# The third layer of a graph network gathers the rows of x itself, instead of reading a copy stored by slot

## The chip, the cores and the metric

The kernel runs on one core of a Trainium2 chip. The metric is the time on the device in microseconds (us), the median of several runs. A core has five engines, each with its own instruction queue, which run side by side and wait for one another through semaphores: TensorE (PE; its weight loads are listed as PEld), VectorE (DVE), ScalarE (ACT), GpSimd (POOL) and SyncE (SP, which here only issues transfers). Transfers between HBM and the on-chip memory (SBUF) are issued by SP, or, where rows are picked by a list of indices, by POOL as indirect transfers.

## The reference

Three layers of a graph convolution over 20000 nodes with 512 features, 5000 edges sorted by destination, with a residual from layer to layer and from the input:

```python
h = x
residual = 0.0
for Wl, bl, Wr, g, b in params:                 # three layers
    msg = h[src]                                # 5000 rows
    s = segment_sum(msg, dst, 20000)
    cnt = segment_sum(ones, dst, 20000)
    agg = s / maximum(cnt, 1)
    h = residual + agg @ Wl.T + bl + h @ Wr.T
    h = layer_norm(h, g, b)                     # eps 1e-5
    h = where(h >= 0, h, a_prelu * h)
    residual = h
out = layernorm(x + h)                          # no gain or shift
```

## The kernel before

The nodes are renumbered into slots so that nodes that receive edges come first. There are 157 tiles of 128 slots; 40 of them receive messages. Two tiles make a unit, and a layer has 79 units: 59 plain ones and 20 edge units. In each layer 20 plain units come first; then an edge unit and two plain units alternate; one plain unit of a single tile comes last. The three layers run one behind the other as 237 turns of one pipeline, and every engine's program is a loop over the turn T that works on units somewhat ahead of or behind T. The order on each engine is thus written out by hand.

For unit u, TensorE transposes the rows (`turn`, into `ps_t`), and multiplies them as a sum of a high and a low part with split weights: 12 products of 128x512 a tile, and 12 more for a tile that gets messages (`product_self`, `product_mean`, L411). ScalarE takes the high part (`take_high`, L524), fills the accumulators with the bias (`fill`, L553), squares the result (`square`, L533) and forms the variance (`variance`, L543). POOL takes the inverse root (`root`, L690). VectorE takes the low part (`take_low`, L790), applies root and gain (`normal`, L801), adds the shift (`add_shift`, L822) and takes the PReLU (`prelu`, L828). For edge units it also builds comparison matrices (`compare`, L837 and L839), carries sums over tile borders (`carry`, L854) and takes low parts of sums (`take_sum_low`, L862). `normal` of a unit frees its accumulator, which `fill` and then TensorE need two units later.

In layer 3 the output follows. Tile `o_sb` (a ring of 6 buffers of two tiles) holds rows of x; VectorE adds the layer's result to them (`out_sum`, L870, three turns behind TensorE) and forms the mean (`out_mean`); ScalarE squares (`out_square`, L579); POOL's `root` handles the variance of this second normalisation in the same instruction, then forms `omove` (L694); ScalarE normalises (`out_norm`, L586); and POOL scatters the rows to the output, one indirect transfer a tile (`put_out`, L702).

In layer 1 the rows of x come by indirect transfers on POOL, one a tile (`gather_x`, L656), into `hin`. SP stores each unit from `hin` into the HBM tensor `x_by_slot` (`store_x`, L281); POOL waits for that store before it fills the buffer again. In layer 3 SP loads the unit's rows of `x_by_slot` into `o_sb` in one transfer (`load_residual`, L319), once the scatters that read that buffer six units before have landed (`o_put`). SP's order in a turn is `store_x`, `load_h`, `load_residual`, `load_rowtab`, `store_h`. POOL's order in turn T is: `root` (which waits for the variance), `omove`, the scatters of unit T-5, `gather_x` of unit T+3, the message gathers of unit T+3 if it is an edge unit (`gather_messages`, L679), and in layers 1 and 2 the small transfers that build the slot tables.

Of the kernel before, what the change touches and what calls it, by code (L numbers as in the profile page):

```python
# [7 lines left out]
P = 128  # L8
ALU = mybir.AluOpType
ACT = mybir.ActivationFunctionType  # L10
F32 = mybir.dt.float32
# [4 lines left out]
L = 3  # L16
# [6 lines left out]
def reach(eng, sem, count):  # L23

    if count > 0:
        eng.wait_ge(sem, count)  # L26


def build_program(nc, x, wT, bl, g, b, a_prelu, ident_in, const_in, edge_cols_in, edge_last_in, edge_rows_in,
                  edge_no_in, out):  # L30
    N, D = x.shape
# [3 lines left out]
    NT = -(-(N + ET) // P)  # L35
# [5 lines left out]
    UL = len(edge_units) + len(plain_units)  # L41
# [32 lines left out]
    def uses(ring, n, below):  # L74

        return len(range(ring, below, n))

    h_dram = [nc.dram_tensor(f"h{l + 1}_scratch", [NT * P, D], F32).ap() for l in range(L - 1)]
    xp_dram = nc.dram_tensor("x_by_slot", [NT * P, D], F32).ap()
    node_dram = nc.dram_tensor("node_of_rank", [EP, 1], I32).ap()  # L80
    slot_dram = nc.dram_tensor("slot_of_node", [NT * P, 1], I32).ap()
    rowtab_dram = nc.dram_tensor("edge_row_table", [ET, 2 * P], F32).ap()
# [1 line left out]
    with ExitStack() as ctx:  # L84
# [3 lines left out]
        def sem(name):  # L88
            return ctx.enter_context(nc.semaphore(name))


        OB = 6
# [19 lines left out]
        hin = [sb(f"hin{i}", [P, 2, D]) for i in range(3)]  # L112
# [23 lines left out]
        node_get = sb("node_get", [P, NT], I32)  # L136
# [83 lines left out]
        SRC_AHEAD = 6  # L220
# [3 lines left out]
        def stats(T):  # L224
# [19 lines left out]

        x_in = [[sem(f"x_in{i}_{j}") for j in range(2)] for i in range(3)]
        h_in = [sem(f"h_in{i}") for i in range(3)]
        xp_stored = [sem(f"xp_stored{i}") for i in range(3)]
        h_stored = [sem(f"h_stored{i}") for i in range(3)]
        turned, high, low, z_ready = sem("turned"), sem("high"), sem("low"), sem("z_ready")
        squared, veps_done, rstd_done = sem("squared"), sem("veps_done"), sem("rstd_done")  # L250
# [2 lines left out]
        m_in = [sem(f"m_in{j}") for j in range(2)]  # L253
        e_same, e_summed, e_carry, e_high, e_low = (
            sem("e_same"), sem("e_summed"), sem("e_carry"), sem("e_high"), sem("e_low"))
        xr_in = [sem(f"xr_in{i}") for i in range(OB)]
        o_put = [[sem(f"o_put{i}_{j}") for j in range(2)] for i in range(OB)]
        o_summed, o_mean, o_squared = sem("o_summed"), sem("o_mean"), sem("o_squared")
        o_move, o_done = sem("o_move"), sem("o_done")
# [1 line left out]
        def rows(dram, u):  # L261
            return dram[P * u.tiles[0]:P * (u.tiles[0] + u.n), :].rearrange("(j p) d -> p j d", p=P)


        def sync_program(sp):
            def load_weight(w):
                if w == 1:
                    sp.wait_ge(turned, 1)
                if w > 0:
                    sp.wait_ge(w_low, KC * w)  # L270
                sp.dma_start(stage[:], wT[w].rearrange("(c p) k -> p c k", p=P)).then_inc(stage_in, 16)

            def spread(vector, count):
                return vector.rearrange("(a d) -> a d", a=1).to_broadcast([count, vector.shape[0]])

            def store_x(u):
                if u.l > 0:
                    return
                for j in range(u.n):
                    sp.wait_ge(x_in[u.r3][j], 16 * (u.no // 3 + 1))  # L280
                sp.dma_start(rows(xp_dram, u), hin[u.r3][:, 0:u.n, :]).then_inc(xp_stored[u.r3], 16)  # L281

            def load_h(u):
                if u.l == 0:
                    return
                source = u.no - UL
                sp.wait_ge(turned, u.no - 2)
                sp.wait_ge(h_stored[source % 3], 16 * (source // 3 + 1))
                if u.no - 3 < UL:
                    sp.wait_ge(xp_stored[u.r3], 16 * uses(u.r3, 3, UL))  # L290
                sp.dma_start(hin[u.r3][:, 0:u.n, :], rows(h_dram[u.l - 1], u)).then_inc(h_in[u.r3], 16)

            def load_rowtab(u):
                if not u.edge:
                    return
                if u.eno == 0:
                    sp.wait_ge(rowtab_stored, 16)
                reach(sp, e_same, 2 * u.eno)
                t = u.tiles[0]
                pair = rowtab_dram[t:t + 2, :].rearrange("(a t) c -> a (t c)", a=1)  # L300
                sp.dma_start(rowtab[:].rearrange("p j c e -> p (j c e)"),
                             pair.to_broadcast([P, 4 * P])).then_inc(rt_in, 16)

            def store_h(u):
                if u.l == L - 1:
                    return
                sp.wait_ge(h_done, u.no + 1)
                sp.dma_start(rows(h_dram[u.l], u), hout[u.r3][:, 0:u.n, :]).then_inc(h_stored[u.r3], 16)

            def load_residual(u):  # L310
                if u.l < L - 1:
                    return
                if u.pos == 0:
                    sp.wait_ge(z_ready, NT)
                    for r in range(3):
                        sp.wait_ge(xp_stored[r], 16 * uses(r, 3, UL))
                for j in range(2):
                    reach(sp, o_put[u.ring][j], 16 * u.lap)
                sp.dma_start(o_sb[u.ring][:, 0:u.n, :], rows(xp_dram, u)).then_inc(xr_in[u.ring], 16)  # L319

            sp.dma_start(edge_cols[:], edge_cols_in).then_inc(cols_in, 16)
            sp.dma_start(const[:], const_in).then_inc(const_in_sem, 16)
            sp.dma_start(ident[:], ident_in).then_inc(ident_in_sem, 16)
            load_weight(0)
            sp.dma_start(edge_rows, edge_rows_in).then_inc(rows_in, 16)
            sp.dma_start(edge_no, edge_no_in).then_inc(rows_in, 16)
            sp.dma_start(dlast[:], spread(edge_last_in, P)).then_inc(rows_in, 16)
            for l in range(L):
                sp.dma_start(bias_rows[:, l, :], spread(bl[l], P)).then_inc(bias_in, 16)
            sp.dma_start(slope[:], spread(a_prelu, P)).then_inc(affine_in, 16)  # L330
            for l in range(L):
                sp.dma_start(gain[:, l, :], spread(g[l], P)).then_inc(affine_in, 16)
                sp.dma_start(shift[:, l, :], spread(b[l], P)).then_inc(affine_in, 16)
            sp.wait_ge(table_done, 1)
            sp.dma_start(node_dram.rearrange("(t p) c -> t (p c)", p=P), table_int[0:ET, 0, :]).then_inc(node_stored, 16)

            for T in range(-5, UNITS + 3):
                for stage_, ahead in ((store_x, 2), (load_h, 3), (load_residual, -1), (load_rowtab, 5), (store_h, -3)):
                    u = Unit(T + ahead)
                    if u.exists:  # L340
                        stage_(u)
                for w, at in W_SLOT.items():
                    if T == at - 4:
                        load_weight(w)
                if T == ROW_SLOT + 2:
                    sp.wait_ge(row_step, 12)
                    sp.dma_start(rowtab_dram, rows_out.rearrange("t c p -> t (c p)")).then_inc(rowtab_stored, 16)
                if T == TABLE_SLOT + 2:
                    sp.wait_ge(table_done, 3)
                    sp.dma_start(slot_dram[0:P * P, :].rearrange("(t p) c -> t (p c)", p=P),  # L350
                                 table_int[:, 0, :]).then_inc(slot_stored, 16)
                    sp.dma_start(slot_dram[P * P:NT * P, :].rearrange("(t p) c -> t (p c)", p=P),
                                 table_int[0:NT - P, 1, :]).then_inc(slot_stored, 16)
# [285 lines left out]
        def gpsimd_program(pool):  # L639
# [8 lines left out]
            def gather_x(u):  # L648
                if u.l > 0:
                    return  # L650
                reach(pool, turned, u.no - 2)
                reach(pool, xp_stored[u.r3], 16 * (u.no // 3))
                if u.edge:
                    pool.wait_ge(nodes_known, 2 + u.tiles[-1] // BATCH)
                for j, t in enumerate(u.tiles):
                    pool.indirect_dma_start(hin[u.r3][:, j, :], None, x,  # L656
                                            bass.IndirectOffsetOnAxis(node_get[:, t:t + 1], 0)).then_inc(x_in[u.r3][j], 16)

            def find_source(u):
                if not u.edge or u.l != 1:  # L660
# [47 lines left out]
            for T in range(-3, UNITS + 6):  # L708
# [2 lines left out]
                old = Unit(T - 5)  # L711
                if old.exists:
                    put_out(old)
                for stage_, ahead in ((gather_x, 3), (gather_messages, 3), (find_source, SRC_AHEAD)):
                    u = Unit(T + ahead)
                    if u.exists:
                        stage_(u)
# [22 lines left out]
        def vector_program(dve):  # L740
# [123 lines left out]
            def out_sum(u):  # L864
                if u.l < L - 1:
                    return
                dve.wait_ge(xr_in[u.ring], 16 * (u.lap + 1))
                dve.wait_ge(h_done, u.no + 1)
                for j in range(u.n):
                    nc.vector.scalar_tensor_tensor(o_sb[u.ring][:, j, :], hout[u.r3][:, j, :], sign[:, 0:1], o_sb[u.ring][:, j, :],  # L870
                                                   ALU.mult, ALU.add, accum_out=osum[u.ring][:, j:j + 1]).then_inc(o_summed, 1)

# [193 lines left out]
```

## Time and profile before

| what | value |
|---|---|
| median of 3 runs | 2023.56 us (2023.55 to 2024.12) |
| profiled execution | 2023.93 us, of which the span is 2022.1 |
| busy share of the span | PE 98%, PEld 82%, DVE 79%, ACT 60%, POOL 46% |
| TensorE in the 40 slices of the span | 90% busy or more in slices 2 to 39 |
| `gather_x` on POOL (L656) | 157 calls, mean 1001 ns, 3.8 us from issue to landing |
| `put_out` on POOL (L702) | 157 calls, mean 1039 ns, 2.9 us from issue to landing |
| store of a unit into `x_by_slot` | 512 KB, 3.3 us from issue to landing |
| load of a unit from `x_by_slot` | 512 KB, 4.6 us from issue to landing |

A "busy" engine is one with an instruction in hand. The idle time in front of an instruction is given with what ended it (`<-`). "Issue" is idle time in which the engine waited for nothing the profile shows. Layer 1 takes about the first 695 us, layer 2 the time to about 1335, layer 3 the rest.

### The profile page before, as it was taken

The page shows a single profiled execution, that of the slowest core. Times are in us where ns is not written, and L with a number is a line of the kernel's source. Part 1 is how long each engine was busy: PE and PEld are TensorE (multiplying, and loading weights), DVE is VectorE, ACT ScalarE, POOL GpSimd, SP SyncE. Part 2 cuts the span into 40 slices and gives each one's busy share as a digit, 9 for nine tenths or more (in the row PEclk, how much of TensorE's full clock was granted, in tenths as well). Part 3 has the DMA queues.
Part 4 walks back from the last instruction along what each step waited for, and adds up shares of the span by engine and source line. Part 5 has one row for each costly group of instructions (what it writes and reads, how often), then busy time and mean ns, then how long its engine had stood idle before and what let it go on. Part 6 is the DMA issues. An engine that isn't in the chain of part 4 may idle for free. (4 is left out here: it accounts for less than half of the span.)

```text
span 2022.1 us, 30522 instructions
## 1 busy us (share of the span) xinstructions
PE 1978.4 (98%) x10207; PEld 1659.0 (82%) x10207; DVE 1597.5 (79%) x2598; ACT 1221.7 (60%) x2667; POOL 926.7 (46%) x885
## 2 busy tenths in 40 slices
PE   8999999999999999999999999999999999999993
PEld 7888888888888888888888888887788888888882
DVE  7778777777777677777777777779999988888884
ACT  6865554554444455444444444458887777777774
POOL 3666656555565312332222333214555555555554
PEclk9999999999999999999999999999999999999997
DMA  6667667666666555544444444456666666656652
GB/s 209 226 232 258 215 219 233 221 208 214 204 204 207 161 162 183 170 146 152 146 145 151 157 156 144 138 173 216 221 230 217 211 212 213 209 203 218 214 183 92
DMA packets 181075, 387.69 MB, mean 192 GB/s; under 512 B 20117, under 2 KB 20562, under 8 KB 180918
## 3 DMA queue, kind: packets, MB, share of 16 engines
q1 hardware_dynamic: 142358, 272.06, 39.7%
q0 software_dynamic: 38560, 113.67, 17.3%
q8 instruction: 82, 1.34, 0.3%
q14 instruction: 75, 0.61, 0.1%
HBM read 221.07 MB, written 164.79 MB: 191 GB/s over the span
## 5 line engine op out<-in xcount | busy, mean ns | idle before, releaser
L411 PE MATMUL ps_z<-w_hi,hT_hi 128*128 128x512 f32 x1884 | 762.9, 405 | 5.7 <-ACT ps_z L553 4.9
L411 PE MATMUL ps_z<-w_hi,hT_lo 128*128 128x512 f32 x1884 | 738.6, 392 | 0.0
L411 PE MATMUL ps_z<-w_lo,hT_hi 128*128 128x512 f32 x1884 | 737.8, 392 | 0.0
L690 POOL TENSOR_TENSOR rstd<-veps,minus_half 128x2 f32<-128x2 f32 (+1 forms) x240 | 241.6, 1007 | 876.1 <-ACT veps L543 876.0
L790 DVE TENSOR_TENSOR hT_lo<-ps_t,hT_hi 128x1024 fp32r<-128x1024 f32 (+1 forms) x237 | 288.0, 1215 | 320.3 <-ACT hT_hi L524 317.6
L553 ACT COPY ps_z<-bias_rows 128x512 f32<-128x512 f32 x471 | 276.7, 588 | 346.5 <-DVE y L801 334.7
L533 ACT ACTIVATE junk<-ps_z 128x512 f32<-128x512 f32 x471 | 278.6, 592 | 322.3 <-PE ps_z L411 322.1
L411 PEld LDWEIGHTS ps_z<-w_hi,hT_lo 128*128 128x128 f32 x1884 | 353.4, 188 | 79.0
L411 PEld LDWEIGHTS ps_z<-w_hi,hT_hi 128*128 128x128 f32 x1884 | 354.4, 188 | 75.9 <-issue 8.1
L411 PEld LDWEIGHTS ps_z<-w_lo,hT_hi 128*128 128x128 f32 x1884 | 354.8, 188 | 66.9
L801 DVE SCALAR_TENSOR_TENSOR y<-ps_z,rstd,gain 128x512 f32<-128x512 f32 x471 | 330.2, 742 | 4.5 <-POOL rstd L690 4.5
L828 DVE SCALAR_TENSOR_TENSOR hout<-y,slope 128x1024 f32<-128x1024 f32 (+1 forms) x237 | 301.4, 1272 | 0.0
L822 DVE TENSOR_TENSOR y<-y,shift 128x1024 f32<-128x1024 f32 (+1 forms) x237 | 290.5, 1226 | 8.1
L391 PEld LDWEIGHTS ps_t<-ident,hin 128*128 128x128 f32 x1884 | 219.1, 140 | 34.2 <-issue 4.6
L391 PE MATMUL ps_t<-ident,hin 128*128 128x128 f32 x1884 | 244.7, 273 | 0.5 <-DVE hT_lo L790 0.5
L524 ACT CAST hT_hi<-ps_t 128x1024 fp32r<-128x1024 f32 (+1 forms) x237 | 234.7, 990 | 6.2 <-PE ps_t L391 5.9
L702 POOL DMA_INDIRECT out<-o_sb,node_put x157 | 163.1, 1039 | 68.2 <-issue 53.0
L411 PE MATMUL ps_z<-w_hi,sT_lo 128*128 128x512 f32 x480 | 188.0, 392 | 0.0
L411 PE MATMUL ps_z<-w_hi,sT_hi 128*128 128x512 f32 x480 | 187.7, 391 | 0.0
L411 PE MATMUL ps_z<-w_lo,sT_hi 128*128 128x512 f32 x480 | 187.7, 391 | 0.0
L656 POOL DMA_INDIRECT hin<-in_x,node_get x157 | 157.2, 1001 | 63.5 <-issue 36.2
L586 ACT ACTIVATE o_sb<-o_sb,omove,rstd 128x512 f32<-128x512 f32 x157 | 119.6, 809 | 68.5 <-POOL omove L694 68.5
(144 smaller groups left out, 1928.9 us busy)
## 6 DMA issues: line engine op xcount, KB each, us to landing
h_scratch<-hout SPq DMA_DIRECT2D x156, 512.0 KB, 3.7
hin<-h_scratch SPq DMA_DIRECT2D x156, 512.0 KB, 3.9
x_by_slot<-hin SPq DMA_DIRECT2D x78, 512.0 KB, 3.3
o_sb<-x_by_slot SPq DMA_DIRECT2D x78, 512.0 KB, 4.6
rowtab<-edge_row_table SPq DMA_DIRECT2D x60, 256.0 KB, 3.6
stage<-in_WrT SPq DMA_DIRECT2D x3, 1024.0 KB, 8.2
stage<-in_WlT SPq DMA_DIRECT2D x3, 1024.0 KB, 7.4
hin<-in_x,node_get POOLq DMA_INDIRECT x157, 3.8
```

The source lines that it names most:

```text
L391: mm = pe.transpose(ps_t[:, j, k * P:(k + 1) * P], hin[u.r3][:, j, k * P:(k + 1) * P], ident[:])
L411: mm = pe.matmul(acc, a[:, k, :], ww[:, k, :], start=False, skip_group_check=True, stop=stop and k == KC - 1 and a is a_lo)
L524: nc.scalar.copy(hT_hi[u.r2][:, 0:u.n].rearrange("p j k n -> p (j k n)"), ps_t[:, 0:u.n, :].rearrange("p j d -> p (j d)")).then_inc(high, 1)
L533: nc.scalar.activation(junk[j][:], ps_z[u.r2][:, j, :], ACT.Square, accum_out=ssq[u.r2][:, j:j + 1]).then_inc(squared, 1)
L553: nc.scalar.copy(ps_z[u.r2][:, j, :], bias_rows[:, u.l, :]).then_inc(filled, 1)
L656: pool.indirect_dma_start(hin[u.r3][:, j, :], None, x, bass.IndirectOffsetOnAxis(node_get[:, t:t + 1], 0)).then_inc(x_in[u.r3][j], 16)
L690: nc.gpsimd.tensor_tensor(rstd[(T - 1) % 2][:, at], veps[(T - 1) % 2][:, at], minus_half[:, at], ALU.pow).then_inc(rstd_done, 1)
L702: pool.indirect_dma_start(out, bass.IndirectOffsetOnAxis(node_put[:, t:t + 1], 0), o_sb[u.ring][:, j, :], None, bounds_check=N - 1, oob_is ...
L790: nc.vector.tensor_tensor(hT_lo[u.r2][:, 0:u.n].rearrange("p j k n -> p (j k n)"), ps_t[:, 0:u.n, :].rearrange("p j d -> p (j d)"), hT_hi[ ...
L801: nc.vector.scalar_tensor_tensor(y[u.r2][:, j, :], ps_z[u.r2][:, j, :], rstd[u.r2][:, j:j + 1], gain[:, u.l, :], ALU.mult, ALU.mult).then_ ...
L822: nc.vector.tensor_tensor(y[u.r2][:, 0:u.n, :], y[u.r2][:, 0:u.n, :], moved, ALU.add).then_inc(shifted, 1)
L828: nc.vector.scalar_tensor_tensor(hout[u.r3][:, 0:u.n, :], y[u.r2][:, 0:u.n, :], slope[:, 0:1], y[u.r2][:, 0:u.n, :], ALU.mult, ALU.max).th ...
```

## The change

The HBM copy `x_by_slot` is gone: SP no longer stores x in layer 1 and no longer loads it in layer 3, and POOL's gather of layer 1 no longer waits for a store. In layer 3 POOL gathers the unit's rows straight from the input into `o_sb`, one indirect transfer a tile, in turn T for unit T, after the scatters of the turn and ahead of its message gathers. Each tile of a buffer has a semaphore of its own, for which `out_sum` waits tile by tile.

```diff
-            def store_x(u):
-                if u.l > 0:
-                    return
-                for j in range(u.n):
-                    sp.wait_ge(x_in[u.r3][j], 16 * (u.no // 3 + 1))
-                sp.dma_start(rows(xp_dram, u), hin[u.r3][:, 0:u.n, :]).then_inc(xp_stored[u.r3], 16)
...
-                if u.no - 3 < UL:
-                    sp.wait_ge(xp_stored[u.r3], 16 * uses(u.r3, 3, UL))
...
-            def load_residual(u):
-                if u.l < L - 1:
-                    return
-                if u.pos == 0:
-                    sp.wait_ge(z_ready, NT)
-                    for r in range(3):
-                        sp.wait_ge(xp_stored[r], 16 * uses(r, 3, UL))
-                for j in range(2):
-                    reach(sp, o_put[u.ring][j], 16 * u.lap)
-                sp.dma_start(o_sb[u.ring][:, 0:u.n, :], rows(xp_dram, u)).then_inc(xr_in[u.ring], 16)
...
-                for stage_, ahead in ((store_x, 2), (load_h, 3), (load_residual, -1), (load_rowtab, 5), (store_h, -3)):
+                for stage_, ahead in ((load_h, 3), (load_rowtab, 5), (store_h, -3)):
...
-                reach(pool, xp_stored[u.r3], 16 * (u.no // 3))
...
+            def gather_residual(u):
+                if u.l < L - 1:
+                    return
+                if u.pos == 0:
+                    pool.wait_ge(z_ready, NT)
+                for j, t in enumerate(u.tiles):
+                    reach(pool, o_put[u.ring][j], 16 * u.lap)
+                    pool.indirect_dma_start(o_sb[u.ring][:, j, :], None, x,
+                                            bass.IndirectOffsetOnAxis(node_get[:, t:t + 1], 0)).then_inc(xr_in[u.ring][j], 16)
...
-                for stage_, ahead in ((gather_x, 3), (gather_messages, 3), (find_source, SRC_AHEAD)):
+                for stage_, ahead in ((gather_x, 3), (gather_residual, 0), (gather_messages, 3), (find_source, SRC_AHEAD)):
...
-                dve.wait_ge(xr_in[u.ring], 16 * (u.lap + 1))
                 dve.wait_ge(h_done, u.no + 1)
                 for j in range(u.n):
+                    dve.wait_ge(xr_in[u.ring][j], 16 * (u.lap + 1))
```

## Rows read from the trace of the kernel before

**Rows 1.** Table of stretches, two stretches: busy us and operations of each engine, clock, DMA.

```profile
1357.00:1457.00 100.00, 95.63 (x465) 76.92 (x463) 91.84 (x143) 87.49 (x197) 46.16 (x51) 1.00 0.63 211
1700.00:1800.00 100.00, 100.00 (x519) 84.82 (x519) 91.48 (x172) 79.42 (x170) 53.11 (x55) 1.00 0.60 213
```

**Rows 2.** Groups of instructions on POOL, 1515 to 1960 us.

```profile
L690 POOL TENSOR_TENSOR rstd<-veps,minus_half 128x4 f32<-128x4 f32 x51 | 64.8, 1271 | 149.4 <-ACT veps L543 149.4
L679 POOL DMA_INDIRECT msg<-h_scratch,src_slot x34 | 58.5, 1720 | 10.4 <-issue 10.4
```

**Rows 3.** Timeline of POOL, 1700 to 1762: start us, length us, line, tiles, idle before.

```profile
1705.85 1.39 POOL L690 TENSOR_TENSOR rstd<-veps,minus_half 128x4 f32<-128x4 f32 x1 [2.72 <-ACT veps L543]
...
1714.44 1.38 POOL L690 TENSOR_TENSOR rstd<-veps,minus_half 128x4 f32<-128x4 f32 x1 [4.08 <-ACT veps L543]
...
1721.10 1.91 POOL L679 DMA_INDIRECT msg<-h_scratch,src_slot  x1 [0.30 <-issue]
1725.16 1.05 POOL L690 TENSOR_TENSOR rstd<-veps,minus_half 128x4 f32<-128x4 f32 x1 [2.16 <-ACT veps L543]
...
1727.06 1.06 POOL L702 DMA_INDIRECT out<-o_sb,node_put  x1 [0.58 <-issue]
1728.43 0.98 POOL L702 DMA_INDIRECT out<-o_sb,node_put  x1 [0.30 <-issue]
1732.13 1.39 POOL L690 TENSOR_TENSOR rstd<-veps,minus_half 128x4 f32<-128x4 f32 x1 [2.72 <-ACT veps L543]
```

**Rows 4.** Timeline of VectorE, same stretch.

```profile
1709.93 1.22 DVE L822 TENSOR_TENSOR y<-y,shift 128x1024 f32<-128x1024 f32 x1
...
1712.11 1.28 DVE L828 SCALAR_TENSOR_TENSOR hout<-y,slope 128x1024 f32<-128x1024 f32 x1
...
1718.69 1.23 DVE L822 TENSOR_TENSOR y<-y,shift 128x1024 f32<-128x1024 f32 x1
...
1720.88 1.28 DVE L828 SCALAR_TENSOR_TENSOR hout<-y,slope 128x1024 f32<-128x1024 f32 x1
...
1722.94 0.75 DVE L870 SCALAR_TENSOR_TENSOR o_sb<-hout,sign,o_sb 128x512 f32<-128x512 f32 x1
...
1727.22 1.40 DVE L801 SCALAR_TENSOR_TENSOR y<-ps_z,rstd,gain 128x512 f32<-128x512 f32 x2
1728.66 1.22 DVE L822 TENSOR_TENSOR y<-y,shift 128x1024 f32<-128x1024 f32 x1
1729.80 1.28 DVE L828 SCALAR_TENSOR_TENSOR hout<-y,slope 128x1024 f32<-128x1024 f32 x1
```

**Rows 5.** Timeline of POOL in the plain part, 1400 to 1430.

```profile
1407.24 1.37 POOL L690 TENSOR_TENSOR rstd<-veps,minus_half 128x4 f32<-128x4 f32 x1 [2.71 <-ACT veps L543]
...
1414.45 1.20 POOL L690 TENSOR_TENSOR rstd<-veps,minus_half 128x4 f32<-128x4 f32 x1 [2.71 <-ACT veps L543]
...
1421.50 1.38 POOL L690 TENSOR_TENSOR rstd<-veps,minus_half 128x4 f32<-128x4 f32 x1 [2.71 <-ACT veps L543]
...
1425.04 0.97 POOL L702 DMA_INDIRECT out<-o_sb,node_put  x1 [0.30 <-DVE y L801]
```

**Rows 6.** Timeline of VectorE, 1405 to 1425.

```profile
1425.00 1.29 DVE L822 TENSOR_TENSOR y<-y,shift 128x1024 f32<-128x1024 f32 x1
```

**Rows 7.** Timeline of POOL: first edge units, and the end.

```profile
1457.14 1.21 POOL L690 TENSOR_TENSOR rstd<-veps,minus_half 128x4 f32<-128x4 f32 x1 [2.71 <-ACT veps L543]
...
1514.92 1.05 POOL L690 TENSOR_TENSOR rstd<-veps,minus_half 128x4 f32<-128x4 f32 x1 [0.87 <-ACT veps L543]
...
1987.53 1.04 POOL L690 TENSOR_TENSOR rstd<-veps,minus_half 128x4 f32<-128x4 f32 x1 [5.78 <-ACT veps L543]
```

**Rows 8.** Groups of TensorE by form, 670 to 694.

```profile
L411 PE MATMUL ps_z<-w_lo,hT_hi 128*128 128x512 f32 x20 | 7.9, 395 | 0.0
```

**Rows 9.** Groups of TensorE by form, 700 to 724.

```profile
L411 PE MATMUL ps_z<-w_lo,hT_hi 128*128 128x512 f32 x31 | 12.1, 390 | 0.0
```

**Rows 10.** Instructions on the tensor x_by_slot: ns min/median/max, first and last start.

```profile
L281 SPq DMA_DIRECT2D x_by_slot<-hin x79: 332/359/377, 27.2 to 668.9; - x79
```

More of the change, by code:

```diff
@@ L78, in build_program @@
     h_dram = [nc.dram_tensor(f"h{l + 1}_scratch", [NT * P, D], F32).ap() for l in range(L - 1)]
-    xp_dram = nc.dram_tensor("x_by_slot", [NT * P, D], F32).ap()
     node_dram = nc.dram_tensor("node_of_rank", [EP, 1], I32).ap()
@@ L246, in build_program @@
         h_in = [sem(f"h_in{i}") for i in range(3)]
-        xp_stored = [sem(f"xp_stored{i}") for i in range(3)]
         h_stored = [sem(f"h_stored{i}") for i in range(3)]
@@ L255, in build_program @@
             sem("e_same"), sem("e_summed"), sem("e_carry"), sem("e_high"), sem("e_low"))
-        xr_in = [sem(f"xr_in{i}") for i in range(OB)]
+        xr_in = [[sem(f"xr_in{i}_{j}") for j in range(2)] for i in range(OB)]
         o_put = [[sem(f"o_put{i}_{j}") for j in range(2)] for i in range(OB)]
```

## The prediction, made before the result was known

> **What bounds the kernel now.** I read the table of stretches first: it says which engine is full in which layer. In the third layer's steady part TensorE is busy for the whole stretch at a granted clock of 1.00 (the upper level, 2.4 GHz), VectorE 91%, ScalarE 79%, GpSimd (POOL) 53%; in its first part, where only plain units run, TensorE falls to 95.6% [rows 1]. The change puts all its new work on POOL in this layer, so the next view is POOL's groups there: its only real idle time is the wait of `root` (L690) for ScalarE's variance, 149.4 us before 51 roots, and the message gathers cost 1720 ns each, against 0.97 to 1.06 us for an undisturbed call [rows 2, 3]. The third view is POOL's order of time. From one edge unit to the next there are three steps, root to root: A (1705.85 to 1714.44), B (to 1725.16, with two message gathers) and C (to 1732.13), 26.28 us together, with 4.08, 2.16 and 2.72 us free in front of the next root [rows 3]. The 17 such periods between 1515 and 1960 have 149.4/17 = 8.79 us free each [rows 2]. So POOL has slack now, but not much.
>
> The fourth view sets VectorE's order beside it, since a POOL call that begins inside certain VectorE operations is long. The message call at 1721.10 began inside `prelu` (L828, both inputs in SBUF, 1720.88 to 1722.16), took 1.91 and ended 0.85 after it [rows 3, 4]. Calls beginning beside operations that read PSUM (`normal`, L801) take 0.97 to 1.06 [rows 3]. I take it that a call begun inside an operation with two SBUF inputs (`add_shift` L822, `prelu` L828, `out_sum` L870, `take_sum_low` L862) ends 0.85 after it, and any other takes 0.97.
>
> **The change part by part.** *Removed in layer 1*: 79 stores of x by slot and SP's and POOL's waits on them. TensorE is full there (table of the profile above), so nothing is behind them: 0. *Removed in layer 3*: 79 loads on SP's queue, for which no one waits: 0. The traffic of the loads stays, on another queue. *Data in time*: a gather of x lands 3.8 us after issue (same table); POOL issues unit u's in step u and VectorE reads it in turn u+3, more than two steps later (over 14 us): 0. The new wait on `o_put` is for a scatter issued one step earlier, long landed: 0. *Added*: 157 calls on POOL, two in each step, behind the two scatters and ahead of the message gathers. Behind them on POOL waits the next root; for it wait `normal` on VectorE and, through `omove`, ScalarE's `out_norm`, `fill` and squares, and so the next variance. The chain closes on itself, so a root that is late by POOL's own length makes the layer as long as the sum of POOL's steps.
>
> Bounds of a pair of calls, each with its 0.30 gap: 2 x (0.30+0.97) = 2.54 at the least, 2 x (0.30+1.72) = 4.04 by the message gathers. A period takes three pairs: 7.62 to 12.12 against 8.79 free. The value depends on where each call falls, so I walk through POOL's loop as it is once a root waits for POOL alone. From the end of a root the first scatter starts at +0.85 and the second at +2.22 [rows 3]. VectorE's `normal` starts just after the root (+0.05) or, if the root was on time, 2.06 after the root's start (1725.16 to 1727.22); `add_shift` comes 1.44 after `normal` and lasts 1.23; `prelu` starts 1.14 after it in C, and 2.19 in B and A, where the compares or a carry of about that length stand between; the second `out_sum` starts 2.06 after `prelu` and lasts 0.75 [rows 3, 4].
>
> Step C: `add_shift` +1.49 to +2.72, so the second scatter (+2.22) ends at +3.57; first gather at +3.87, as `prelu` ends (+3.92): free, to +4.84; second at +5.14 inside the second `out_sum` (to +5.45), to +6.30. With the root (1.05) 7.35, now 6.97.
> Step A: an on-time root stands 5.92 after the end of C's root (1726.21 to 1732.13), so this one is 0.38 late and `normal` starts 0.63 after its end. `add_shift` +2.07 to +3.30: scatter to +4.15; `prelu` +4.25 to +5.53: first gather (+4.45) to +6.38; second `out_sum` to +7.06: second gather (+6.68) to +7.91. With the root 8.96, now 8.59.
> Step B: root 1.2 (behind L862), `normal` about +0.26, `add_shift` to +2.93: scatter to +3.78; `prelu` to +5.17: first gather to +6.02; second `out_sum` to +6.70: second gather to +7.55; the two messages now meet free time, 2.54, to +10.09. With the root 11.3, now 10.72.
> Sum 27.6 against 26.28: 1.3 us a period, 17 x 1.3 = 22.5 us.
>
> Plain part: two steps take 14.26 now (1407.24 to 1421.50), 7.13 each, with 2.71 free, just over 2.54 [rows 5]. The same walk gives steps of 7.35 and, where the root is 0.45 late (its own chain: 1415.65 to 1421.50, 5.85), 7.86: +0.47 a step over 11 steps, and 1.1 for the first late root: 6 us. First edge units: seven steps from 1457.14 to 1514.92 take 57.8 now [rows 7]; a plain step with two messages (7.6+2.54) and two periods of 27.6 make 65.3: 7.5 us. End: the last steps C and A cost 0.7; in the last edge unit's step POOL waits 5.78 now [rows 7], has no messages, and 1.5 come back. Sum: 22.5 + 6 + 7.5 + 0.7 - 1.5 = 35 us. The profiled execution took 2023.93 (span 2022.1 and 1.8 around it), 0.4 over the median; 2023.6 + 35 = 2059.
>
> The row on who holds whom: a scatter at 1425.04, just after an `add_shift` that started at 1425.00, took its usual 0.97, and the `add_shift` 1.29 instead of 1.23, so VectorE lost 0.06 [rows 4 to 6]. The Trainium skill (SBUF — State Buffer, section "SBUF: two separate sides") says that the pair of ports which VectorE and GpSimd share is locked by whichever starts first, for its whole instruction. For VectorE in front the trace agrees (the 0.85 above); for GpSimd in front it does not (0.06, not 0.97). By the page's rule VectorE would lose up to 0.97 more beside a call that starts first; that is the third rival.
>
> **The rivals.**
> *The gathers fit.* If POOL's calls find VectorE's PSUM operations, 7.62 of 8.79 is used and only the first edge step (no idle time now) and a few late roots cost: +3 to +7, 2027 to 2031. Between this and my sum lies the case that the scatter of step A, only 0.15 inside `add_shift`, escapes it: A is then bound by ScalarE's chain (7.20 from root to root) at 8.25, 0.7 less a period, +23, 2047. For it: the same calls in layer 1 average 1.0 us (same table). Against: there they come first behind the root, where VectorE runs `normal`; here they start two calls later. Fit: 0.14; the escape is part of the forecast.
> *All calls as long as messages.* 12.12 - 8.79 = 3.3 a period, 57; 1.33 x 11 = 15 in the plain part; some 11 in the first edge units: +83, 2107. Against: two of my six calls fall free. Something between is likelier. 0.12.
> *GpSimd locks VectorE too.* Two free gathers a period, each delaying VectorE by 0.97, beyond the sum: 17 x 1.9 = 33 more, 2092. The 0.06 speaks against it. 0.03.
> *Faster: the stores slow the products.* In layer 1 a 128x512 product takes 395 ns, in layer 2 390 [rows 8, 9], and layer 1 is where x is stored. 12 for each of 157 tiles and of 40 message tiles, 2364, by 5 ns are 12 us. It decides the sign if those go and the gathers fit: 2017. Against: the last store is issued at 668.9, and from 670 to 694, with none left, it is still 395 [rows 8, 10]; the step stands at the change of layer, with its weights. 0.05. Were the x gathers its cause, layer 3 would slow by as much; the same row speaks against that.
>
> **How the numbers follow.** Forecast 0.66 (own range 2045 to 2075), fit 0.14, long calls 0.12, lock 0.03, faster 0.05. The range 2031 to 2085 leaves out half of the fits, the faster case and the longest of the long calls, about 0.18. What a measurement can tell from no change is 0.2%, 4 us: the fits are within it two times in five. Faster 0.05, within 0.06, slower 0.89.
>
> **What would show it.** Right: in layer 3 roots that start when POOL's last call ends, with almost no idle time in front of roots; gathers of two kinds, near 0.97 and up to 1.95, ending 0.85 after an L822, L828 or L870; a period near 27.6; TensorE near 95% there (26.28/27.6); layers 1 and 2 unchanged. Wrong: `root` still idle by 1 us a period, gathers all near 1.0, a changed product time in layer 1, or `out_sum` waiting for a DMA.

## The result, and the profile after

The changed kernel takes 2054.49 us (median of four runs, 2054.08 to 2054.57), the kernel before 2023.55 beside it: ratio 1.0152, 95% interval 1.0134 to 1.017. The profiled spans are 2052.7 and 2022.1 us, 30.6 apart. The forecast was 2059.

Read the stretches first, as before: busy us of PE, PEld, VectorE, ScalarE and POOL, then clock, DMA share and GB/s.

```profile
1357.00:1457.00 100.00, 91.47 (x446) 73.70 (x445) 87.30 (x138) 82.83 (x186) 73.28 (x76) 1.00 0.64 203
1700.00:1800.00 100.00, 97.62 (x497) 82.12 (x496) 88.50 (x165) 74.21 (x163) 80.52 (x73) 1.00 0.61 195
```

Against [rows 1], POOL gained 27 us of work in each 100, and TensorE, VectorE and ScalarE all lost some. No other engine has more to do: they wait. TensorE's granted clock is still 1.00 (2.4 GHz) in both stretches, so the lost time is waiting and not a lower clock. (Ahead of the layer's end the clock fell once, to 1.2 GHz from 1475.6 to 1479.0, just after TensorE had stood idle for 2.6 us: the first edge unit's messages, gathered later in the turn now, landed at 1475.5. No idle time stands before the roots around it, so neither shows in the time of a step.) Who waits for whom stands in the groups of POOL from 1545 to 1990 us (count | busy us, mean ns | idle before, with its releaser):

```profile
L643 POOL DMA_INDIRECT o_sb<-in_x,node_get x97 | 131.8, 1359 | 29.6 <-issue 29.6
L689 POOL DMA_INDIRECT out<-o_sb,node_put x98 | 128.1, 1307 | 46.4 <-issue 45.5 <-ACT o_sb L564 0.9
L677 POOL TENSOR_TENSOR rstd<-veps,minus_half 128x4 f32<-128x4 f32 x49 | 55.5, 1132 | 0.6
L666 POOL DMA_INDIRECT msg<-h_scratch,src_slot x32 | 30.5, 952 | 9.8 <-issue 9.8
```

The wait of `root` (now L677), 149.4 us before 51 roots in [rows 2], is down to 0.6 before 49. POOL is no longer waiting for anyone. The scatters became longer (1039 ns over the layer before, 1289 after) and the message gathers shorter (1720, now 952): how long a call is depends on where it falls. On the other side of the wait, `normal` on VectorE, before and after, and `out_norm` on ScalarE after, in the same stretch:

```profile
L801 DVE SCALAR_TENSOR_TENSOR y<-ps_z,rstd,gain 128x512 f32<-128x512 f32 x102 | 71.5, 743 | 3.5 <-POOL rstd L690 3.5
L788 DVE SCALAR_TENSOR_TENSOR y<-ps_z,rstd,gain 128x512 f32<-128x512 f32 x98 | 68.8, 743 | 48.6 <-POOL rstd L677 48.6
```

```profile
L564 ACT ACTIVATE o_sb<-o_sb,omove,rstd 128x512 f32<-128x512 f32 x98 | 74.6, 808 | 117.9 <-POOL omove L681 117.9
```

Both now wait for POOL: `normal` 48.6 us instead of 3.5, `out_norm` 117.9 instead of 41.7.

And the fourth part of the page, the chain that ended last, by engine and by line:

```profile
POOL 21%; issue 10%; ACT 0%; POOLq 0%; ACTq 0%
POOL o_sb L643 9%; POOL out L689 5%; POOL rstd L677 4%; POOL msg L666 2%; POOL omove L681 1%; POOLq L689 0%; ACT o_sb L564 0%; ACT stage L557 0%; ACT junk L511 0%; ACT veps L521 0%; ACT ps_z L531 0%; POOLq L724 0%; POOLq L676 0%; ACTq L26 0%; POOLq L26 0%
```

POOL and the gaps in this chain in which nothing is waited for ("issue", for the most part those between POOL's calls) are 31% of the span. The third layer is (2052.7 - 1335) / 2052.7 = 35% of it, so the chain runs through nearly all of the layer; in the kernel before it reaches back over no more than the last few turns. One period, root to root, shows the three steps C, A and B of the walk. POOL first (start, length):

```profile
1720.18 1.05 POOL L677 TENSOR_TENSOR rstd<-veps,minus_half 128x4 f32<-128x4 f32 x1
...
1722.09 1.05 POOL L689 DMA_INDIRECT out<-o_sb,node_put  x1 [0.58 <-issue]
1723.44 1.36 POOL L689 DMA_INDIRECT out<-o_sb,node_put  x1 [0.31 <-issue]
1725.10 0.99 POOL L643 DMA_INDIRECT o_sb<-in_x,node_get  x1 [0.30 <-issue]
1726.40 1.04 POOL L643 DMA_INDIRECT o_sb<-in_x,node_get  x1 [0.31 <-issue]
1727.45 1.07 POOL L677 TENSOR_TENSOR rstd<-veps,minus_half 128x4 f32<-128x4 f32 x1
...
1730.72 1.93 POOL L689 DMA_INDIRECT out<-o_sb,node_put  x1 [0.30 <-issue]
1732.96 1.95 POOL L643 DMA_INDIRECT o_sb<-in_x,node_get  x1 [0.30 <-issue]
1735.21 1.13 POOL L643 DMA_INDIRECT o_sb<-in_x,node_get  x1 [0.30 <-issue]
1736.34 1.26 POOL L677 TENSOR_TENSOR rstd<-veps,minus_half 128x4 f32<-128x4 f32 x1
...
1745.34 0.95 POOL L666 DMA_INDIRECT msg<-h_scratch,src_slot  x1 [0.30 <-issue]
1746.59 0.95 POOL L666 DMA_INDIRECT msg<-h_scratch,src_slot  x1 [0.30 <-issue]
1747.57 1.05 POOL L677 TENSOR_TENSOR rstd<-veps,minus_half 128x4 f32<-128x4 f32 x1
```

and VectorE's operations beside the calls of step A:

```profile
1730.57 1.22 DVE L809 TENSOR_TENSOR y<-y,shift 128x1024 f32<-128x1024 f32 x1
...
1732.74 1.28 DVE L815 SCALAR_TENSOR_TENSOR hout<-y,slope 128x1024 f32<-128x1024 f32 x1
...
1734.73 0.75 DVE L857 SCALAR_TENSOR_TENSOR o_sb<-hout,sign,o_sb 128x512 f32<-128x512 f32 x1
```

Every root starts as the last call in front of it ends (1726.40 + 1.04 = 1727.44, root at 1727.45). The steps are 7.27, 8.89 and 11.23 us, 27.39 a period, where 6.97, 8.59 and 10.72 (26.28) stood. In step A three of the four calls begin inside a VectorE operation with two SBUF inputs and end shortly after it: the second scatter at 1732.65, 0.86 after `add_shift` (1731.79); the first gather at 1734.91, 0.89 after `prelu` (1734.02); the second at 1736.34, 0.86 after `out_sum` (1735.48). Of the 157 gathers of x in the layer 148 began inside such an operation and ended 0.82 to 0.99 after it; the nine others took 0.99 on average. One that begins in the last tenth, as at 1725.10, is no longer than a free one.

### The profile page after: what moved, and what is told of

The parts are those of the page before. It is cut to its first block and busy times, and to the rows that moved or that the text cites. A ratio compares the mean times of both kernels' runs of the same rounds, so it can differ in the third digit from the quotient of the medians.

```text
span 2052.7 us, 30312 instructions
## 1 busy us (share of the span) xinstructions
PE 1986.8 (97%) x10207; PEld 1663.4 (81%) x10207; DVE 1600.9 (78%) x2598; ACT 1212.3 (59%) x2667; POOL 1125.7 (55%) x1042
## 5 line engine op out<-in xcount | busy, mean ns | idle before, releaser
L677 POOL TENSOR_TENSOR rstd<-veps,minus_half 128x2 f32<-128x2 f32 (+1 forms) x240 | 230.9, 962 | 659.4 <-ACT veps L521 658.4
L809 DVE TENSOR_TENSOR y<-y,shift 128x1024 f32<-128x1024 f32 (+1 forms) x237 | 290.3, 1225 | 8.1
L689 POOL DMA_INDIRECT out<-o_sb,node_put x157 | 202.3, 1289 | 72.4 <-issue 71.0
L643 POOL DMA_INDIRECT o_sb<-in_x,node_get x157 | 201.4, 1283 | 47.2 <-issue 47.1
```

The source lines that it names most:

```text
L643: pool.indirect_dma_start(o_sb[u.ring][:, j, :], None, x, bass.IndirectOffsetOnAxis(node_get[:, t:t + 1], 0)).then_inc(xr_in[u.ring][j], 16)
L677: nc.gpsimd.tensor_tensor(rstd[(T - 1) % 2][:, at], veps[(T - 1) % 2][:, at], minus_half[:, at], ALU.pow).then_inc(rstd_done, 1)
L689: pool.indirect_dma_start(out, bass.IndirectOffsetOnAxis(node_put[:, t:t + 1], 0), o_sb[u.ring][:, j, :], None, bounds_check=N - 1, oob_is ...
L809: nc.vector.tensor_tensor(y[u.r2][:, 0:u.n, :], y[u.r2][:, 0:u.n, :], moved, ALU.add).then_inc(shifted, 1)
```

## The experiments

**Theory:** the third layer is now as long as POOL's own list of calls, and a call's length is set by the VectorE operation that it begins in. **Rivals:** the layer waits for memory traffic or late data; the time hangs on the number of calls alone; the removed stores gave or took something.

**The stores kept.** The changed kernel, with layer 1's stores of x by slot and the waits on them put back.

```diff
+                for stage_, ahead in ((store_x, 2), (load_h, 3), (load_rowtab, 5), (store_h, -3)):
+                reach(pool, xp_stored[u.r3], 16 * (u.no // 3))
```

> The changed kernel with the stores of x by slot in layer 1 put back; nothing reads the copy. Theory (the removed stores had nothing behind them): 2054 us within 2. Rival (their removal gained something that the gathers' price hides): longer than the changed kernel by what they cost, up to 12 us, 2066.

2054.74 us, ratio 1.0153 (1.0124 to 1.0183): the stores cost nothing. The products of layer 1 show why no gain came from them; from 600 to 640 us, without stores, the changed kernel has

```profile
L389 PE MATMUL ps_z<-w_lo,hT_hi 128*128 128x512 f32 x34 | 13.4, 395 | 0.0
```

the same 395 ns as in [rows 8], so whatever makes them longer than layer 2's 390 is not the store.

**The calls without the traffic.** The kernel before, with two further indirect transfers in each turn of layer 3, in the place of the new ones, of four bytes a row into a scratch column that nothing reads. SP's stores and loads stay.

```diff
+            def gather_tiny(u):
...
+                for t in u.tiles:
+                    pool.indirect_dma_start(tiny[:, t:t + 1], None, slot_dram,
+                                            bass.IndirectOffsetOnAxis(edge_cols[:, 2, t % ET:t % ET + 1], 0)).then_inc(tiny_in, 16)
```

> The kernel before (x stored by slot and loaded by SP), with two more indirect gathers on POOL in each turn of layer 3, in the place where the change puts its gathers, but of 4 bytes a row into a scratch tile that nothing reads. Theory (POOL's own time in its calls closes the loop root to root): the same as the changed kernel, 2050 to 2058 us, steps of about 7.3, 8.9 and 11.2 us, no idle time before the roots. Rival (the 40 MB of picked rows on POOL's queue, their landing or their traffic): almost no bytes are added, so 2024 us.

2059.64 us, ratio 1.0178 (1.0148 to 1.0207), steps 7.34, 8.89 and 11.29. The time sits 1.6 us over the range given for POOL's time and far from the traffic's 2024. Its groups from 1545 to 1960:

```profile
L665 POOL DMA_INDIRECT tiny<-slot_of_node,edge_cols x92 | 128.4, 1396 | 28.1 <-issue 28.1
L699 POOL TENSOR_TENSOR rstd<-veps,minus_half 128x4 f32<-128x4 f32 x45 | 50.9, 1131 | 0.6
```

Two transfers that move 512 bytes each, with SP's loads in place as they were, cost no less than gathers of 256 KB. It is POOL's time for the call, not the data. The span is 4.9 us longer than the changed kernel's, and the traces say where: 2.5 lie in the 17 periods, where this run still has the old waits of `out_sum` (see the term that was mis-sized, below), 0.6 in the turns before them, and 1.8 in layer 1, where the new scratch column moves the weights and the products take 396 and 397 ns instead of 395 (see the part on the weights). Nothing is left for the removed loads of layer 3.

**Half the dose.** One gather a unit by POOL; SP loads the unit's other tile from the copy.

```diff
-                for j, t in enumerate(u.tiles):
+                for j, t in enumerate(u.tiles[:1]):
...
+                sp.dma_start(o_sb[u.ring][:, 1, :], xp_dram[P * t:P * (t + 1), :]).then_inc(xr_in[u.ring][1], 16)
```

> Only the first tile of a unit is gathered by POOL in layer 3; the second comes from the copy by slot, which is kept and loaded by SP as before. Theory: three more calls a period of at most 2.25 us each with their gap, 6.75, stay under the 8.79 free, so the period falls back to about 26.3 us and only the first edge units lose something: 2024 to 2031 us, with over 2 us of idle time before the roots of a period. Rival (every call costs its share, 31 us over 157 calls): 2039 us.

2027.0 us (2025.69 to 2027.59), ratio 1.0015 (1.0004 to 1.0026); the period is back at 26.28. In the same groups:

```profile
L668 POOL DMA_INDIRECT o_sb<-in_x,node_get x48 | 63.3, 1319 | 14.6 <-issue 14.6
L702 POOL TENSOR_TENSOR rstd<-veps,minus_half 128x4 f32<-128x4 f32 x47 | 57.9, 1232 | 71.1 <-ACT veps L545 71.1
```

Half of the calls cost 3 us, all of them 31. Roots have 71.1 us left before 47 of them, 1.51 each; before it was 149.4 / 51 = 2.93 [rows 2]. One call a unit took 1.42 of the slack and cost next to nothing in time; the second takes the other half and more. This is the shape of a resource with slack, and it excludes a price per call.

**Shorter operations on VectorE.** The changed kernel with `add_shift` and `prelu` of layer 3 issued tile by tile, so that a call is held by an operation of half the length. The control is the kernel before with the same edit.

```diff
+                if u.l == L - 1:
+                    for j in range(u.n):
+                        ins = nc.vector.tensor_tensor(y[u.r2][:, j, :], y[u.r2][:, j, :], shift[:, u.l, :], ALU.add)
+                    ins.then_inc(shifted, 1)
+                    return
...
+                    for j in range(u.n):
+                        ins = nc.vector.scalar_tensor_tensor(hout[u.r3][:, j, :], y[u.r2][:, j, :], slope[:, 0:1],
+                                                             y[u.r2][:, j, :], ALU.mult, ALU.max)
```

> The changed kernel with VectorE's add_shift and prelu of layer 3 issued tile by tile, two operations of 512 instead of one of 1024; POOL's calls are as many as in the changed kernel. Theory (a call that begins inside a VectorE operation with two SBUF inputs is held to that operation's end): held calls are held half as long, the longest fall from 1.95 to about 1.5, POOL's sum falls under TensorE's time, a period is 26.3 to 26.6 us: 2026 to 2034 us, though VectorE gets more instructions. Rival (the calls are long by themselves in layer 3, or their count alone matters): 2054 us or a little more.

> The kernel before with add_shift and prelu of layer 3 issued tile by tile: the control for the split kernel. Theory (the split helps only by freeing POOL's calls sooner, and POOL is not late here): 2023 to 2026 us. Rival (the split saves time on VectorE or TensorE by itself): under 2020 us.

The changed kernel falls to 2032.01 us, ratio 1.0042 (1.0022 to 1.0061); the control stays at 2024.82, 1.0005 (0.9994 to 1.0015). POOL's calls are the same in number, and none of its own instructions was touched, yet 22.5 of the 31 us are gone. Its groups from 1545 to 1960:

```profile
L643 POOL DMA_INDIRECT o_sb<-in_x,node_get x95 | 112.4, 1183 | 28.9 <-issue 28.9
L689 POOL DMA_INDIRECT out<-o_sb,node_put x94 | 101.3, 1077 | 43.6 <-issue 42.7 <-ACT o_sb L564 0.9
L677 POOL TENSOR_TENSOR rstd<-veps,minus_half 128x4 f32<-128x4 f32 x48 | 60.1, 1252 | 11.5 <-ACT veps L521 11.1
```

Calls of 1359 and 1307 ns became 1183 and 1077, the longest gather fell from 2.03 to 1.54 us, and some idle time stands before roots again. Where the rest of the loss lies is seen in the stretches 1400 to 1500 and 1500 to 1900:

```profile
1400.00:1500.00 100.00, 90.49 (x435) 72.90 (x434) 89.04 (x168) 81.26 (x180) 77.90 (x82) 0.98 0.67 217
1500.00:1900.00 400.00, 400.00 (x2076) 339.47 (x2075) 367.45 (x763) 309.70 (x671) 306.45 (x304) 1.00 0.64 210
```

From 1500 TensorE is full again; what is left of the loss lies ahead of it, in the plain part (11 steps 81.1 us, 78.4 before) and the first edge units (62.6, 57.8 before): 2.7 + 4.8 = 7.5 of the 8. POOL is the limit there still: from 1387 to 1522 its roots have 1.5 us of idle time before 17 of them. The clock of 0.98 comes from one stretch at 1.2 GHz, 1474.2 to 1477.6, after TensorE had stood idle for 3.3 us until the first messages landed; no loss can be seen from it, since a run without such a stretch (gathers first and split, below) has first edge units of 62.8.

**The gathers ahead of the scatters.** The same calls in the other order, right behind `omove`.

```diff
+                if 0 <= T < UNITS:
+                    gather_residual(Unit(T))
                 old = Unit(T - 5)
...
-                for stage_, ahead in ((gather_x, 3), (gather_residual, 0), (gather_messages, 3), (find_source, SRC_AHEAD)):
+                for stage_, ahead in ((gather_x, 3), (gather_messages, 3), (find_source, SRC_AHEAD)):
```

> The changed kernel with POOL's two gathers of x put ahead of the two scatters in each turn of layer 3. Theory (what counts is the place of a call beside VectorE, not what it moves): the scatters now take the long places, and the sum is the same, 2050 to 2058 us; the first call after a root is short (1.05) whatever it is. Should the gather have to wait for the scatter of the turn before, which lands some 2.9 us after its issue, up to 1 us a turn more, 2130. Rival (gathers of x are long in layer 3 by themselves): they keep their mean of 1.28 us and their long calls of 1.95 stand in the first place too.

2046.17 us, ratio 1.0111 (1.009 to 1.0131): 8 less than in the order of the change, and 3.8 below the range given. The calls changed places as expected: 147 of the 157 scatters now begin inside a VectorE operation with two SBUF inputs (73 in the change), and 54 of the gathers (148). So the gathers are not long by themselves; their mean alone, 1.26 us over the layer, would not have told. The sum was not the same, though. Steps A are of two kinds here, 7.95 and 8.88, and POOL's timeline shows the start of a short one:

```profile
1724.19 1.06 POOL L677 TENSOR_TENSOR rstd<-veps,minus_half 128x4 f32<-128x4 f32 x1
...
1725.68 1.02 POOL L643 DMA_INDIRECT o_sb<-in_x,node_get  x1 [0.16 <-issue]
1727.01 0.97 POOL L643 DMA_INDIRECT o_sb<-in_x,node_get  x1 [0.30 <-issue]
1728.28 1.11 POOL L689 DMA_INDIRECT out<-o_sb,node_put  x1 [0.30 <-issue]
```

A gather stands 0.16 behind `omove` where a scatter stands 0.58, so the second call begins 0.4 earlier and can escape `add_shift` (1727.01 here, `add_shift` at 1727.28). The first rival of the prediction has such an escape and puts it at 2047. The mechanism is like it, the agreement in the number is luck: the rival had every step A at 8.25, 0.7 less a period; here 9 of 17 are at 7.95, seven of them in periods of 26.2 instead of 27.5, and the others gain nothing. Why only some escape is open. The order of equal work thus moves the time by 8 us.

**Both, with the weights moved** (the last edit is the subject of the next part).

> The changed kernel with three edits together: the gathers of x ahead of the scatters, add_shift and prelu of layer 3 issued tile by tile, and 96 bytes ahead of layer 1's weights. By the theory (a turn of POOL's work is longer than TensorE's period only because calls are held by VectorE operations with two SBUF inputs) the gathers then fall beside normal, the calls held are held by less, the plain part and the first edge units lose at most half of the 8 us that the split alone left, and the place of the weights gives 8.6 to 13: 2013 to 2022. By the rival (the 8 us left are the calls' own time, whatever their place) 2019 to 2024.

2031.54 us, ratio 1.0039 (1.0025 to 1.0053): I was wrong, under both readings. The larger part of the miss is the place of the weights, which I put at 8.6 to 13 and which gives 2.3 with 96 bytes (next part). The rest is the early gathers: 2032.0 - 2.3 would be 2029.7, so beside the split they cost 1.8 instead of giving something. POOL's groups in 1350 to 1460 show a wait that this expectation left out (that of the run before had named it):

```profile
L644 POOL DMA_INDIRECT o_sb<-in_x,node_get x30 | 31.4, 1048 | 13.8 <-DMA out<-o_sb,node_put 8.0 <-issue 5.2 <-ACT o_sb L565 0.3
```

The gather fills the buffer that the scatters of the turn before have read. In the order of the change it is issued some 10 us after them (scatter at 1396.15, gather of the next turn at 1406.47 in the split kernel); moved ahead, in turns of 7 us, some 4 us after (1397.62 and 1401.56 here), and a scatter takes 4.6 us from issue to landing. The calls are short (1048 ns) and POOL idles instead, for 38.3 us in all between 1545 and 1960. With the order alone moved the same wait is 19.3 us over the whole layer. Unlike the `o_put` wait that I set at 0 in the change, it counts here.

**Where the weights of layer 1 lie.** The 395 ns had no cause yet. Layer 1's weights are in a region of their own; an unused tile ahead of them moves them (and `o_sb`, which shares their place and which layer 1 doesn't use) and nothing else. Four sizes, in the kernel before:

```diff
+        sb("pad", [P, 8])       # 32 bytes; 16, 24 and 120 for 64, 96 and 480
         early = ExitStack()
         for w in range(2):
             w_hi[w], w_lo[w] = sb(f"w_hi{w}", wide, F32R, early), sb(f"w_lo{w}", wide, F32R, early)
```

> The kernel before with 32 unused bytes a partition placed ahead of the weights of layer 1, so that they start at a multiple of 64 bytes, as those of layers 2 and 3 do, and no longer 32 past one. It tests the cause of layer 1's slower products, which the prediction's fourth rival laid to the stores. Theory (where layer 1's weights lie): products of layer 1 at 390 to 391 ns instead of 395, 12 to 14 us less, 2010 to 2012 us. Rival (the transfers of layer 1, gathers and stores, slow them): 395 ns and 2023.6 us.

> The kernel before with 96 bytes put ahead of layer 1's weights instead of 32. Theory (the products of layer 1 are slow because of where their operands begin in SBUF, and 32 bytes cured only a part): now all three 128x512 products of layer 1 take 390 ns as in layer 2, 2009 to 2012. Rival (32 bytes gave all that the place of the operands can give, the rest is something else of layer 1): as with 32 bytes, 2015. Rival (the gain with 32 bytes came from o_sb or another buffer that moved along, not from the weights): anything up to 2024.

> The kernel before with 64 bytes ahead of layer 1's weights (0 gave products of 395 ns, 32 gave 390 for w_lo and 393 for w_hi, 96 gave 394 and 395). Theory (the place of the weights decides, and a start at an odd multiple of 32 bytes is what costs): as 96 bytes or as 0 (0, 64 put the start at the same remainder by 64), 2020 to 2024. Rival (only some distance to the other operands counts and every step of 32 differs): a third time, anywhere from 2010 to 2024, with products between 390 and 395.

> The kernel before with 480 bytes ahead of layer 1's weights: they then begin at the same remainder by 512 as the weights of layers 2 and 3, whose products take 390 ns. Theory (the remainder by 512 of the weights' start decides): all products of layer 1 at 390, 2010 to 2012. Rival (the distance between the weights and the other operand decides, which differs from that of layers 2 and 3 still): 2015 to 2024.

| bytes ahead | w_lo x hT_hi, w_hi x hT_lo in 600 to 640 us, ns | time, us | ratio (95%) |
|---|---|---|---|
| 0 | 395, 395 | 2023.7 | 1 |
| 32 | 390, 393 | 2015.05 | 0.9957 (0.994 to 0.9973) |
| 64 | 395, 396 | 2024.14 | 1.0002 (0.9992 to 1.0012) |
| 96 | 394, 395 | 2021.6 | 0.9989 (0.9979 to 0.9998) |
| 480 | 390, 391 | 2011.32 | 0.9937 (0.9921 to 0.9954) |

The groups of the kernel with 480 bytes, 600 to 640 us:

```profile
L412 PE MATMUL ps_z<-w_hi,hT_lo 128*128 128x512 f32 x40 | 15.6, 391 | 0.0
L412 PE MATMUL ps_z<-w_lo,hT_hi 128*128 128x512 f32 x40 | 15.6, 390 | 0.0
```

The cause of the 395 is the place of the weights: with 480 bytes layer 1 is as fast as layer 2, and the kernel before gains 12.4 us, the 12 us that the prediction's fourth rival had computed from 5 ns a product, though it laid them to the stores. All of it falls in layer 1, which takes 650.0 us from its first transposition to layer 2's instead of 662.6; layers 2 and 3 are the same within 0.2, so `o_sb` has no part in it. I expected 32 bytes to be the whole cure (2010 to 2012), then 96; both were wrong. The addresses are the program's layout and stand in no trace. In the kernel before the weights begin at byte 195744 of a partition, 32 more than a multiple of 64; 32, 96 and 480 bytes all bring them to a multiple of 64, and 96 is nearly as slow as 0, so that is not the rule. 64 bytes came out as expected, like 0, but by a theory that the 96 had already refuted. The 480 bytes were chosen for 195744 + 480 = 383 x 512 + 128, the remainder by 512 at which the later layers' weights begin (16512 = 32 x 512 + 128), and that run came out as forecast. One hit does not make the remainder by 512 the rule; which distance TensorE cares about is open.

The version with 480 bytes beats both kernels. With the split and 32 bytes the changed kernel reaches the time of before:

> The changed kernel with both the split and the 32 bytes. Both theories together: 2032 less 13, 2018 to 2020 us, so faster than the kernel before although without the copy by slot. If layer 1's products are not cured by the place of the weights, 2032.

2023.22 us, ratio 0.9996 (0.9986 to 1.0006), over the range given by what the 32 bytes fell short: they give 2023.73 - 2015.05 = 8.7 in the kernel before, and 2032.0 - 8.7 = 2023.3. The two edits add, and what the change costs beside the split stays.

## Why the prediction was right

The mechanism is the one forecast: POOL's own length takes the place of its wait for the variance. Term by term, us, roots taken from both traces:

| step of the prediction | forecast | measured |
|---|---|---|
| steps C, A, B | 7.35, 8.96, 11.3 | 7.27, 8.89, 11.23 |
| 17 periods | +22.5 | 465.67 - 446.76 = +18.9 |
| plain part, 11 steps | +6, steps 7.35 and 7.86 | 84.04 - 78.40 = +5.6, steps 7.30 and 7.83 |
| first edge units | +7.5 | 65.71 - 57.78 = +7.9 |
| end | +0.7 - 1.5 | 23.65 - 25.85 = -2.2 |
| stores, loads, data in time | 0 | what is left of the spans' 30.6, +0.4 |
| sum | +35 | +30.6 |

**Bounds of a pair of calls.** A pair costs between 2.54 and 4.04. A period before had 8.79 us free and is 1.11 longer now: (8.79 + 1.11) / 3 = 3.30 for each pair. This is net: the scatters became longer and the messages shorter. It is neither end, so a mean price from one row would have given the wrong sign of the residue (fit) or three times its size (long calls, 3.3 a period); the walk, call by call against VectorE's order, gave it.

**The term that was mis-sized: the period, 1.33 forecast, 1.11 measured**, which makes 3.6 us over 17 periods. The walk let the second `out_sum` start 2.06 after `prelu`, as in [rows 4] (1720.88 to 1722.94). After, it is 1.99 (1732.74 to 1734.73), and the last gather of a step is held by it. The change did this itself: its diff gives `out_sum` other waits, the data first before, `h_done` first and then a semaphore for each tile after. Of the runs without the split, all with the old waits have 0.10 us between `prelu` and the first `out_sum`, and all with the new ones 0.04, with half of the calls as with all. The run of four-byte transfers has the old waits and all of the calls:

```profile
1736.30 1.28 DVE L838 SCALAR_TENSOR_TENSOR hout<-y,slope 128x1024 f32<-128x1024 f32 x1
1737.68 0.75 DVE L880 SCALAR_TENSOR_TENSOR o_sb<-hout,sign,o_sb 128x512 f32<-128x512 f32 x1
```

Its steps C and B are 7.34 and 11.29, as the walk had them, and its 17 periods take 468.1 us, 2.5 more than after. The other 1.1 lie in step A, 8.89 in both: with the old waits `normal` begins 0.55 after the end of the late root there, where the walk had 0.63. Which part of the new waits shortens the gap, the order or the semaphore for each tile, was not tried.

**The end** was better too. In the last edge unit's turn POOL had 5.78 us in front of it [rows 7]. After, POOL fills this turn with its own calls and does not wait (7.50 us against 10.29; the root at its end starts 0.66 us behind its variance): 2.8 come back, not 1.5.

**The zeros held.** Stores: shown by the run that kept them, and layer 3's first transposition starts at 1333.1 us before and 1333.2 after. Data in time and the wait on `o_put`: no time of the gathers' idle goes to a DMA in the groups above; the runs with moved gathers show what the lead behind the scatters is worth.

**One sign read differently.** TensorE was to be busy near 95% of the time. It is 97.6% busy from 1700 to 1800, but with 497 products and transpositions in place of 519, which is 95.8%. The same operations are counted with a little more busy time, so the count shows the loss and the busy share hides part of it.

**The lock.** The rival that GpSimd also stops VectorE is out: from 1545 on, where two more calls stand in every turn, `add_shift` has a mean of 1225 ns before and after, `prelu` 1279 and 1278, `out_sum` 749 and 750. More directly, 276 of VectorE's operations with two SBUF inputs begin in layer 3 of the changed kernel while an indirect transfer's call is running, and none is longer for it (37 `prelu` at 1278 ns, the 42 others at 1277). The row that the prediction gives for GpSimd in front does not show that case: `add_shift` starts at 1425.00 and the scatter at 1425.04, so VectorE is first by 0.04. Such near ties came out both ways; a call that started 0.05 behind the `add_shift` at 1382.25 took 2.02. The Trainium skill (SBUF — State Buffer, section "SBUF: two separate sides") describes an exclusive lock on the ports that VectorE and GpSimd share, held by whoever came first for its whole instruction. For VectorE in front, with two SBUF inputs, this case agrees (gathers up to 2.03 us, ended 0.82 to 0.99 after the operation, shorter as soon as that operation was halved). For an indirect transfer's call in front the measurement decides against it: VectorE's operations did not lengthen.

## What to carry to other kernels

An engine with idle time in each step can take more work until that idle time is used up, and not beyond: 1.42 us a unit cost 3 us in all, 3.30 a unit cost 31. Work out where each added call falls against the operations that hold it, since the same four calls in a turn took 4.44 us in step C and 6.05 in step A by their place alone, and halving two operations on another engine gave back 22.5 us. A transfer by list of indices on GpSimd is paid in that engine's time for the call, whatever it moves; a plain load on SP was free here. And look at what else a diff changes: the new waits of `out_sum` are worth 2.5 us here, by the two runs that differ in them.

## What was not expected of the hardware

The time of a 128x512 fp32 product depends on the byte at which the weights begin in SBUF: 395 ns or 390, with intermediate cases in which one operand pair is cured and another only in part. Over layer 1 that is 12.4 us, 0.6% of this kernel, for an unused tile of 480 bytes a partition. The granted clock is 1.00 there in both. And a small call is not cheaper than a large one: an indirect transfer of 4 bytes a row took 1396 ns of POOL's time, of 2048 bytes a row 1359, in the same place of the turn; the nine of each kind that began outside such a VectorE operation took 0.99 us.
